# Graph layer with gathers paced by look-ups: the allowance of six tiles ahead is set to none

## The reference

```python
h = maximum(layernorm(x), 0)
e = concatenate([h[src], h[dst], edge_attr], -1)      # 400000 x 96
v = relu(e @ W1 + b1) @ W2 + b2                       # 64 hidden, 32 out
out = x + maximum(segment_max(v, dst), h)
```

## Time and profile before

| what | value |
|---|---|
| median of 3 timed runs | 3181.32 us (3181.28 to 3182.08) |
| span of the profiled execution, first to last instruction | 4798.8 us |
| PE, PEld busy in it | 3796.5 us (79%), 2547.3 us (53%) |
| DVE, ACT, POOL busy in it | 2178.1, 2192.4, 2386.6 us (45 to 50%) |
| indirect transfers issued by POOL | 2514 |

### The profile page before, as it was taken

How to read it: one execution, slowest core, us unless ns; L and a number is a source line. 1 busy time by engine, 2 the same in 40 slices (tenths; PEclk the granted TensorE clock), 3 DMA queues, 4 the chain that set the end, 5 groups by cost and what they waited for, 6 DMA issues and landing times.

```text
span 4798.8 us, 56874 instructions
## 1 busy us (share of the span) xinstructions
PE 3796.5 (79%) x19778; PEld 2547.3 (53%) x19778; DVE 2178.1 (45%) x2474; ACT 2192.4 (46%) x2555; POOL 2386.6 (50%) x2523
## 2 busy tenths in 40 slices
PE   5858788778878877877887788778877887778787
PEld 3536455555555545555555555555555555555465
DVE  4211554445444444544444455444444454445356
ACT  2214454445444444544444445444544454445355
POOL 6653455555455455455545555555455555554310
PEclk8979888888778888888887888888888888888798
DMA  8700222222222222222222222222222222222112
GB/s 255 279 10 25 70 80 88 92 85 61 57 68 63 56 66 69 56 61 68 68 55 63 68 65 61 60 69 68 56 63 68 69 61 56 68 68 68 46 55 56
DMA packets 200553, 350.32 MB, mean 73 GB/s; under 512 B 73791, under 2 KB 124251, under 8 KB 200117
## 3 DMA queue, kind: packets, MB, share of 16 engines
q1 hardware_dynamic: 116638, 303.65, 18.4%
q0 software_dynamic: 80448, 41.33, 6.2%
q10 hardware_dynamic: 3332, 4.01, 0.3%
HBM read 240.36 MB, written 119.78 MB: 75 GB/s over the span
## 4 chain that ended last, share of the span: by engine, by line
PE 60%; issue 19%; another core or an unknown queue 10%; DVE 8%; ACT 2%; DMA 0%; DVEq 0%; ACTq 0%; SPq 0%
PE ps_rows L938 38%; PE ps_layers L968 8%; PE ps_layers L963 5%; DVE onehot L1250 3%; PE ps_layers L918 2%; PE ps_layers L953 2%; PE ps_layers L912 2%; DVE max_t L1318 2%; PE ps_layers L957 2%; PE ps_layers L1006 1%; DVE src_t L1285 1%; DVE rows_in L1323 1%; ACT onehot L852 0%; DVE dst_t L1305 0%
## 5 line engine op out<-in xcount | busy, mean ns | idle before, releaser
L664 POOL DMA_INDIRECT src_in<-h_dram,src_ix x2269 | 2147.7, 947 | 1951.5 <-PE ps_rows L938 976.5
L938 PE MATMUL ps_rows<-onehot,table 128*128 128x512 f32 x9898 | 2553.2, 418 | 109.0 <-issue 89.3
L938 PEld LDWEIGHTS ps_rows<-onehot,table 128*128 128x128 f32 x9898 | 1986.6, 203 | 728.8 <-issue 292.8
L852 ACT ACTIVATE onehot<-distance 128x1024 fp32r<-128x1024 bf16 x909 | 905.0, 1049 | 855.0 <-PE ps_rows L938 607.3
L847 ACT ACTIVATE distance<-picks,below_column 128x1024 bf16<-128x1024 int16 x909 | 985.1, 1139 | 0.7 <-DMA picks<-picks_dram 0.7
L838 ACT ACTIVATE hid<-ps_layers,b_col 128x512 f32<-128x512 f32 (+1 forms) x404 | 241.6, 680 | 1407.9 <-remote 912.0
L1300 DVE STREAM_TRANSPOSE ps_layers<-rows_in 128x512 f32<-128x512 f32 x202 | 133.3, 706 | 1561.3 <-ACT hid L838 1561.2
L968 PE MATMUL ps_layers<-picked_rows,w_src 128*64 128x128 f32 x1552 | 399.9, 390 | 550.1 <-issue 545.7
L1250 DVE SCALAR_TENSOR_TENSOR onehot<-picks,column,ps_layers 128x1024 fp32r<-128x1024 int16 x404 | 499.8, 1258 | 310.2 <-PE ps_rows L938 164.7
L968 PEld LDWEIGHTS ps_layers<-picked_rows,w_src 128*64 128x64 f32 x1552 | 188.8, 180 | 784.9 <-issue 782.2
L1318 DVE TENSOR_TENSOR_SCAN max_t<-mask_in,max_t,ps_layers 128x512 f32<-128x512 bf16 x196 | 249.0, 1271 | 337.2 <-remote 331.4
(11 more groups left out here) (145 smaller groups left out, 1283.1 us busy)
## 6 DMA issues: line engine op xcount, KB each, us to landing
picks<-picks_dram SPq DMA_DIRECT2D x101, 512.0 KB
first_rows<-hid SPq DMA_DIRECT2D x100, 500.0 KB
rows_in<-in_edge_attr_dram SPq DMA_DIRECT2D x96, 512.0 KB
rows_in<-first_rows SPq DMA_DIRECT2D x96, 512.0 KB
run_max<-rows_in SPq DMA_DIRECT2D x96, 512.0 KB
src_in<-h_dram,src_ix POOLq DMA_INDIRECT x2269
mask_in<-mask_dram SPq DMA_DIRECT2D x96, 256.0 KB
h_dram<-h_sb ACTq DMA_DIRECT2D x4, 392.0 KB, 5.9
```

The lines of the kernel that those rows point to most:

```text
L664: pool.indirect_dma_start(out=src_in[:, slot, g, r, :], out_offset=None, in_=rows[:, :], in_offset=bass.IndirectOffsetOnAxis(ap=src_ix[:, ...
L852: nc.scalar.activation(onehot[:, RING_AT[c] + BY_DVE[c] + k, :, :].rearrange("p g w -> p (g w)"), distance[:, k, :], ACT.Relu, bias=1.0, s ...
L938: mm = nc.tensor.matmul(ps_rows[g][side][:, 0:WIDE], table[:, i * SIDES + side, part, :], onehot[:, RING_AT[c] + t, g, :], start=(i + part ...
```

## The change

One constant changes. `tiles_before` rises by six for every pair from 7 on, so each of the 12 bursts of a pair waits for six more tiles. Before, bursts 0 to 6 of pair p needed nothing beyond the look-ups of pair p - 6, which are all done when PE starts layer one of pair p - 7, and bursts 7 to 11 needed tiles 1 to 5 of the next look-ups. Now burst 0 needs the look-ups of pair p - 6 complete, and bursts 1 to 11 need tiles 1 to 11 of the next look-ups. The seven pairs that are gathered before the loop, the scatters and the fetches of maxima are not paced by it.

```diff
 BURST = 2
-SLACK = 6
+SLACK = 0
 BURSTS = 2 * GATHERS // BURST
```

## The result

| | time |
|---|---|
| before, median of 6 runs on the same chip | 3181.3 us |
| after, median of 6 runs | 3192.92 us (3190.15 to 3194.95) |
| ratio, 95% interval | 1.0034 (1.0024 to 1.0044): 11.6 us slower, between 7.6 and 14.0 |

The forecast was 3192.0 us. By the bound that the prediction set for itself, 0.2%, the change made the kernel slower.

A forecast was written before the change was run, and what follows sets the result against it. The prediction took POOL's gathers, 1.25 us apart, to bound the timed run; 11 us of POOL idle time in pair 7 added to 3181.3 us gave 3192 us, with later pairs costing nothing. The range was 3165 to 3198 us.

The forecast's parts named there:

- The bound: POOL's gathers bound the timed run, losing about 2.7 us a pair to PE; PE waits in the last third.
- The spacing of 1.25 us: POOL's gathers start 1.25 us apart without a profiler too, so 24 of them take 30.0 us a pair.
- The sum by POOL: Kernel before: start, 2149 gathers at 1.25 us, last turn, one-hot step, pair 96 and end give 3186 us.
- the start of pair 0 at 389 us: Layer one of pair 0 begins at about 389 us in a timed run, 107 us earlier than profiled.
- The step behind POOL's last gather: After the last gather, a slot turn of 1.6 us and a one-hot step of 2.45 us, then pair 96.
- The sum by PE: Kernel before: start at 389 us, 97 pairs at 27.27 us and 87 us of end give 3121 us.
- The first paced pair: In pair 7 POOL's burst 1 waits for the next look-ups' first tile: 11 us idle, bounds 10.2 to 14.6.
- A steady pair costs nothing: Later pairs: no cost, as POOL is behind its gates or, if ahead, has time to spare through its lead.
- Where the loss goes: At the run's end: POOL gathers pair 96 later by 11 us, and PE, waiting for it, ends as much later.
- That POOL makes the loss up: Rival: PE or its partners bound the timed run, so POOL recovers the loss; 3181 to 3183 us, chance 0.34.
- a real trickle: Rival: gathers beside layer one slow PE in timed runs too, so moving them gains up to 51 us; chance 0.16.
- A wait that comes back in each pair: Rival: each pair loses something, 0.2 us in 90 pairs, 18 us on top of 11, 3210 us; chance 0.04.

The follow-up runs named there:

- experiment 7: Kernel before with the last gather of the second half left out, 23 of 24 gathers in each paced pair: 3154.63 us, ratio 0.9913.
- second profile of the kernel before: The kernel before, unchanged, profiled once more: 3182.06 us timed, ratio 1.000, with no stretched work in its profile.
- experiments 5: Kernel before with an allowance of two tiles: 3188.82 us, ratio 1.0021; with pair 7 alone waiting for 19 tiles more: 3222.94 us, ratio 1.0128.
- experiment 1: The kernel before, unchanged, timed and profiled once more: 3182.06 us, ratio 1.000.
- experiment 4: Changed kernel with pairs 7 to 20 at the old allowance of six tiles, later ones at none: 3193.24 us against 3186.75 for the kernel before, ratio 1.0023.
- Experiments 3: Changed kernel with pair 7 alone at the old allowance of six tiles: 3190.15 us, ratio 1.0025 to the kernel before.
- experiment 8: Kernel before with IX_AT = 6 instead of 4, so SP loads the gathers' next indices two pairs later: 3182.94 us, ratio 1.0002.
- two of my repairs: Kernel before with DVE turning pairs 0 to 13 earlier: with 19 tiles 3185.96 us, ratio 0.9998; with six tiles 3185.00 us, ratio 0.9996.
- the one that lasted until PE had quickened: Kernel before with 19 tiles and DVE's early turns going on to pair 28: 3170.64 us against 3181.14, ratio 0.9970.
- the two other kernels that gate pair 7 as strictly or more: Kernel before with pair 7 alone at no allowance: 3193.97 us, ratio 1.0035; with pair 7 alone waiting for 19 tiles more: 3222.94 us, ratio 1.0128.

## Why the prediction was right, point by point

**The bound.** POOL's gathers set the time, by 28 us over PE and its loads (experiment 7). The spacing of 1.25 us, one of the two steps named as weakest, held without the stretching: from the fifth gather of pair 7 at 377.04 us to the last one

```profile
3053.92 0.95 POOL L664 DMA_INDIRECT src_in<-h_dram,src_ix  x1 [0.30 <-issue]
```

are 2676.9 us and 2144 gathers, 1.249 us each. In the second profile of the kernel before, from 389.10 to 3040.99 us, it is the same, so the register additions that moved cost nothing. The rule that the prediction took from the Trainium skill (Perfetto Trace Analysis, section GPSIMD Engine Instruction), to go by the spacing of starts and not by the reported span, is borne out: by spans of 0.95 us POOL would have had time to spare, and experiments 5 and 7 show that it has none.

**The sum by POOL.** Its 3186 us was near for partly wrong reasons. The other weakest step, the start of pair 0 at 389 us, was 25 us late. PE's first layer one in the changed kernel, which answers to the earlier trace rows; in the kernel before it begins at 364.26:

```profile
364.29 2.02 PE L953 MATMUL ps_layers<-ea_t,w_edge 32*64 32x512 f32 x16 [6.98 <-DVE onehot L1250]
366.05 1.96 PE L957 MATMUL ps_layers<-dst_t,w_dst 32*64 32x512 f32 x16
367.75 1.19 PE L963 MATMUL ps_layers<-src_t,w_src 32*64 32x384 f32 x16
...
369.90 7.55 PE L938 MATMUL ps_rows<-onehot,table 128*128 128x512 f32 x32
```

The step behind POOL's last gather was mis-sized the other way. I let PE wait for that gather and begin pair 96 some 4 us later. These rows of POOL, DVE and PE are from the kernel before:

```profile
3004.10 0.85 DVE L1285 STREAM_TRANSPOSE src_t<-src_in 128x384 f32<-128x384 f32 x1 [6.66 <-DMA src_in<-h_dram,src_ix]
3007.54 2.02 PE L953 MATMUL ps_layers<-ea_t,w_edge 32*64 32x512 f32 x16 [3.87 <-DVE onehot L1250]
3040.99 0.94 POOL L664 DMA_INDIRECT src_in<-h_dram,src_ix  x1 [0.31 <-issue]
3063.48 1.11 PE L953 MATMUL ps_layers<-ea_t,w_edge 32*64 32x512 f32 x16
3090.74 0.66 PE L980 MATMUL ps_layers<-ea_t,w_edge 32*64 32x256 f32 x8
```

Pair 96 begins at 3063.48, 22.5 us after the last gather: the last turn that waits for gathers is that of pair 94 (at 3004.10; PE begins the pair at 3007.54), and PE comes to pairs 95 and 96 without waiting for POOL. What I put behind that was right: 27.3 us for pair 96 and 87.5 us from the first small pair to the end of the span, against 27 and 87. So 25 us too many at the start and 18 too few near the end left the sum 5 us from the measured time; that it came so near is luck.

**The sum by PE.** 3121 us was 34 us short of the 3155 of experiment 7, although it too began pair 0 late, by 23 us in that trace. The 97 pairs together take 49 us more than 97 times 27.27, 29 of the 49 in pairs 4 to 12, for the picks; from the first small pair to the end are 87.4 us, as put. That PE isn't slowed by gathers was right: a pair in mid-run takes 27.28 us beside them (experiment 1).

**The first paced pair.** The place and the gate were right: burst 1 of pair 7 waits for the first tile of the next look-ups. The size was near: 11 us taken, 10.2 to 14.6 as bounds, 12.2 us of wait measured, and 12.9 us of idle time more in all. What lay between the bounds is in the rows above: layer one took 5.61 us (364.29 to 369.90) and not the 3.57 of the earlier trace rows. Its first two lines ran at half the granted clock, which they and the third have back in mid-run (columns as in experiment 4):

```profile
364.29:367.70 3.41, 3.41 (x32) 1.17 (x40) 3.16 (x5) 3.41 (x5) 0.00 (x0) 0.50 0.26 104
1301.65:1304.20 2.55, 2.55 (x50) 0.95 (x49) 2.39 (x5) 2.55 (x4) 1.94 (x3) 1.00 0.34 118
```

0.50 is the lower of the two levels, 1.2 GHz; PE had been idle for 6.98 us before it. That is the 2.0 us by which layer one was longer.

**A steady pair costs nothing.** Right for this change, wrong as a rule. I wrote that a wait of a POOL that is ahead costs time that it has to spare. Experiments 3 and 4 refute that: POOL was ahead of its gate at pair 8 and at pair 21, and the waits there went into the end (9.7 and 9.2 us of idle time more, 7.9 and 6.5 us of time). POOL has nothing to spare at any time, because each us of its lead is used up in the last third of the run. In the changed kernel the later pairs cost nothing because pair 7's wait had already set POOL back: no gather behind it waits longer than 0.3 us.

**Where the loss goes.** That all of it reaches the end was right. PE's time from layer one of pair 60 to that of the first small pair shows it: 1052.2 us before (2038.59 to 3090.74), 1064.8 in the changed kernel (2039.39 to 3104.16), 12.6 us more. That PE would wait for the turn of the last slot was only one form: mostly it waits through SP's queue and the picks behind it (experiment 8), at two places after 2250 us in the kernel before and three in the changed one, and last for the turn of pair 94.

**What the profile was to show.** The third gather of pair 7 waits 12.2 us, as said. Waits of POOL's gathers for look-ups grow from 68.5 to 87.0 us and those for turned slots shrink from 3.8 to 0.3, as said. The shorter span and the lesser trickle in L963 and L968 are no evidence: the second profile of the kernel before has no trickle either.

**The rivals.** That POOL makes the loss up falls with experiments 5 and 7, a real trickle with 1. A wait that comes back in each pair is in no trace of a kernel with all its gathers. In experiment 7, where POOL needs less time than PE's slow pairs, it is: at seven slots in a row up to 749 us POOL waits 1.3 to 2.7 us for the turn.

## What to carry to other kernels

Work that bounds a run in its last part has no time to spare earlier, however far ahead it is when it waits: in the changed kernel POOL had a lead of six pairs at 380 us, and from 2250 us on PE stood for its gathers. Look for every stretch in which the bounding engine stands still, above all ahead of the steady state, and check after a repair that the wait hasn't moved to the next gate; two of my repairs lost all or most of what they gained that way, and only the one that lasted until PE had quickened kept its 10.5 us. And when a profiled execution is far from the timed runs, profile once more before taking durations from it.

## What the hardware showed that I hadn't expected

One execution of an unchanged program was profiled at a span of 4798.8 us and the next at 3178.2 us. In the first, layer one trickled beside the gathers; in the second it took 3.57 us as it did without them. No run here shows what made the difference.

In the changed kernel the second gather of burst 1 in pair 7, which waits for no semaphore of its own, came 2.98 us after the first (372.81 and 375.79), 1.73 us later than gathers do; in the two other kernels that gate pair 7 as strictly or more it was the same, in the kernel before 0.34 us. It is in the sums above; its cause wasn't tried.
